# Router logits of four token tiles at once on four column tiles, turned back by a transpose; the feed-forward stage written out without a loop

## The chip, the cores and the metric

The kernel runs on one core of a Trainium2 chip. The metric is the device time in microseconds (us) of one execution, the median of three. The engines that the text speaks of are PE (TensorE, matmuls), PEld (its weight loads), DVE (VectorE), ACT (ScalarE), POOL (GpSimd) and SP (SyncE, which starts transfers). Each engine works through its own instructions strictly in the order written and waits on semaphores for the others.

## The reference

Eight sequences of 1024 tokens with 128 channels pass through a Mamba2 mixer with a small feed-forward layer, then through a top-2 mixture of eight experts. The part that the change touches is the end of the first block and the router's product:

```python
    # end of the first block, h = 128 channels a token
        out = y + residual
        h = layernorm(out, ln_w, ln_b)
        h = jax.nn.relu(h @ mlp_w1 + mlp_b1) @ mlp_w2 + mlp_b2   # 128 -> 512 -> 128
        return h + out
    ...
    x = x + _layernorm(_L0_attn_ref(...))
    # second block: the router sees the normalised x
        x = x_btd.reshape(N, Dm)                                  # _layernorm(x), 8192 tokens
        probs = jax.nn.softmax(x @ Wr + br, axis=-1)              # Wr is 128 x 8
        gates, ids = jax.lax.top_k(probs, K)
```

## The kernel before

The program is a row of stages; at the end of each all engines meet. The first builds the normalised and transposed x, the second is the scan of the mixer, and the third, whose tiles are named `m_...`, is the feed-forward stage that the change rewrites. After it come routing (`r_...`) and the experts (`e_...`).

The feed-forward stage handles 8192 tokens as 64 tiles of 128, two tiles (a group, g = 0 to 31) at a time. A group goes through a chain of steps on four engines. The order of work on each engine is a software pipeline: every engine has a list of pairs (lag, step), and in iteration i it runs, in the order of its list, each step for group i - lag. The 32 groups with a largest lag of 13 make 45 iterations. `skewed` writes iterations 0 to 15 out with constant waits and addresses, then runs iterations 16 to 31 as a hardware loop over a body of eight iterations (so the loop turns back once, after iteration 23), and writes the last 13 out again. In the loop the values of waits and some addresses come from registers.

The lists, in the order of each engine, with the lines of the program before:

- ACT: `centre_x` (lag 0, L1159, writes `m_res`), three square roots `root` (lags 1, 7, 10, L1150, `m_sd`), `turned` (3, L1165, `m_hT` from PSUM `m_pT`), `turned_xl` (12, L1179, `m_xlT` from `m_pX`), `relus` (4, L1172, four of them, `m_h` from `m_pH`).
- DVE: `mlp_out` (6, L1242, `m_at` from `m_pM`), `residual` (0, L1229, two instructions, `m_h` from `arena` and `m_res`), three sets of `bn_stats` and `bn_aggr` (L1195, L1203), three reciprocals (L1263), `apply0`, `apply1`, `apply2` (lags 2, 8, 11, all at L1209, writing `m_hn`, `m_un`, `m_xl`), `logit` (13, L1257, `logits` from `m_pL`).
- PE: `down` (5, L1296, 16 passes into `m_pM`), `up` (3, L1287, 8 passes into `m_pH`), `route` (12, L1311, 4 passes into `m_pL`), `turn` (2, L1278, `m_pT`), `turn_xl` (11, L1304, `m_pX`).
- POOL: `residual_bias` (0, L1128), `add_x` (8, L1132, `arena` from `m_un`), `keep` (11, L1136).

A float32 matmul shows in the trace as two MATMUL records (two passes), a transpose as one. Numbers are dropped from the names of tiles: `m_h<-arena` is the residual `h0`, `m_h<-m_pH` the hidden layer `h1`. Each of PSUM `m_pT`, `m_pX`, `m_pL`, `m_pH` has one copy, most tiles in SBUF four.

The waits between the engines that the prediction uses: `residual(g)` waits for `centre_x(g)`; `turn(g)` for `apply0(g)`; `turn_xl(g)` for `apply2(g)`; `up(g)` for `turned(g)`; `route(g)` for `turned_xl(g)` and for `logit(g-1)`, which empties `m_pL`.

Of the kernel before, what the change touches and what calls it, by code (L numbers as in the profile page):

```python
# [27 lines left out]
ALU = mybir.AluOpType  # L28
ACT = mybir.ActivationFunctionType
AX = mybir.AxisListType  # L30

P = 128
# [64 lines left out]
def build(nc, x, ln_w, ln_b, in_proj_w, conv_w, conv_b, dt_bias, A_log, D_skip, rms_w, out_proj_w,  # L97
# [4 lines left out]
    with ExitStack() as ctx:  # L102
        ctx.enter_context(nc.allow_non_contiguous_dma(reason="columns of a few hundred biases, one element a partition"))

        def sb(name, shape, dt=F32):
            return ctx.enter_context(nc.sbuf_tensor(name, shape, dt))
# [38 lines left out]
        w_m2 = sb("w_m2", [P, NF, D])  # L145
        w_r = sb("w_r", [P, EXPERTS])
        mean = sb("mean", [P, TILES])
# [21 lines left out]
        with ExitStack() as st:  # L169
# [51 lines left out]
            def _(sp):  # L221
                for g in range(STEPS):
# [12 lines left out]
                         (w_m2[:, :, :], mlp_w2.rearrange("(c p) d -> p c d", p=P)),  # L235
                         (w_r[:, :], Wr)]
                assert len(loads) == LOADS
# [13 lines left out]
            def _(g_):  # L251
# [12 lines left out]
                def keep(ap, base, step, chan, cmp=ALU.is_ge, fill=0.0):  # L264
                    nonlocal n
                    g_.affine_select(out=ap, in_=ap, compare_op=cmp, fill=fill, base=base,
                                     pattern=[[step, ap.shape[-1]]], channel_multiplier=chan).then_inc(s_mask, 1)
                    n += 1
                    g_.wait_ge(s_mask, n)
# [31 lines left out]
                for c in range(P // CHUNK):  # L301
                    part = causal[:, CHUNK * c:CHUNK * (c + 1)]
                    keep(part, CHUNK * c, 1, -1)
                    keep(part, -CHUNK * c, 0, 1)
                halo(STEPS - 3)
                halo(STEPS - 2)
# [755 lines left out]
        with ExitStack() as st:  # L1062
# [7 lines left out]
            def pst(name, shape=[P, 512]):  # L1070
# [15 lines left out]
            xlT = sbt("m_xlT", [P, NB, N])  # L1086
            pT, pX, pM0, pM1, pL = (pst("m_" + n) for n in ("pT", "pX", "pM0", "pM1", "pL"))
            pM = [pM0, pM1]
# [5 lines left out]
                 "xlT", "pl", "lg", "hn", "extra"))  # L1094
            s_ph2 = sem("m_ph2")
            s_extra2 = sem("m_extra2")
            s_st = [sem(f"m_st{i}") for i in range(3)]
# [6 lines left out]
            def skewed8(eng, stages):  # L1104

                skewed(eng, GROUPS, 8, 16, stages)

# [35 lines left out]
            def _(a):  # L1143
# [32 lines left out]
                def turned_xl(g, m):  # L1176
                    need(a, s_px, g)
                    need(a, s_pl, g, NB)
                    a.activation(xlT[:, m % NB, :], pX[:, 0:N], ACT.Copy).then_inc(s_xlT, 1)  # L1179

                a.activation(sd_y[:, :], ssq[:, :], ACT.Sqrt, bias=eps[:, 0:1], scale=1.0 / INNER).then_inc(s_extra2, 1)
                a.wait_ge(s_r, 2)
                skewed8(a, [(0, centre_x), (1, root(0)), (7, root(1)), (10, root(2)), (3, turned), (12, turned_xl), (4, relus)])

            @block.vector
            def _(v):
# [68 lines left out]
                def logit(g, m):  # L1255
                    need(v, s_pl, g)
                    v.tensor_tensor(tiles(logits, g), pL[:, 0:G * EXPERTS].rearrange("p (a e) -> p a e", e=EXPERTS),  # L1257
                                    brow[:, :].unsqueeze(1).broadcast_to([P, G, EXPERTS]), ALU.add).then_inc(s_lg, 1)
                def invert(n):
# [13 lines left out]
            def _(pe):  # L1273
# [32 lines left out]

                def route(g, m):
                    need(pe, s_xlT, g)
                    need(pe, s_lg, g, 1)
                    for i in range(G):  # L1310
                        ins = pe.matmul(pL[:, EXPERTS * i:EXPERTS * (i + 1)], xlT[:, m % NB, P * i:P * (i + 1)], w_r[:, :], start=True, stop=True)  # L1311
                    ins.then_inc(s_pl, 1)
                skewed8(pe, [(5, down), (3, up), (12, route), (2, turn), (11, turn_xl)])

# [552 lines left out]
```

## Time and profile before

| | us |
|---|---|
| median of three runs | 945.03 (944.18 to 947.79) |
| the profiled execution's own time | 947.09 |
| its span, first to last instruction | 945.4 |
| the feed-forward stage in it, first `m_res` to last `logits` | 365.4 to 536.4 |
| mean granted TensorE clock | 0.835 |

Over the whole span PE is busy for 71%, DVE for 70%, POOL for 49% and ACT for 48%. These shares mix stages with different limits, so the stage itself has to be read: its order by time on each engine, and what ended each wait. Times in rows of a timeline are us from the start of the span.

### The profile page before, as it was taken

How to read it: one execution, taken by the hardware profiler on the slowest of the kernel's cores; microseconds unless marked ns; L12 is line 12 of the kernel's file. 1: busy time of each engine (PE TensorE's matmuls, PEld its weight loads, DVE VectorE, ACT ScalarE, POOL GpSimd, SP SyncE). 2: the span in 40 equal slices, each digit the busy share in tenths (PEclk: the TensorE clock that was granted, in tenths of full speed). 3: DMA queues.
4: the chain of work that ended last, by engine and by line, in shares of the span. 5: the costliest groups of instructions: out<-in, count | busy, mean ns of one | idle time of the engine just before them, and what ended most of it. 6: DMA issues, size and time to landing. Idle time of an engine off the chain costs nothing. (4 is left out here: it accounts for less than half of the span.)

```text
span 945.4 us, 15492 instructions
## 1 busy us (share of the span) xinstructions
PE 670.3 (71%) x4133; PEld 532.5 (56%) x4133; DVE 663.1 (70%) x2367; ACT 455.4 (48%) x1170; POOL 461.1 (49%) x550
## 2 busy tenths in 40 slices
PE   7456999999999993999899411128498777786000
PEld 3225677777777762989899301114397666675000
DVE  7656999999999963699898586789243233332595
ACT  4764566766667654788775200016243323232143
POOL 7502666766667662234333410000577777777233
PEclk8876999999999996999999555555699999989555
DMA  9920000000000005000000057000323222211882
GB/s 218 367 89 1 1 1 1 1 2 1 1 2 1 1 1 154 26 2 2 2 0 1 1 84 98 0 0 0 91 74 76 75 73 75 75 51 50 228 245 71
DMA packets 73232, 52.95 MB, mean 56 GB/s; under 512 B 11744, under 2 KB 67048, under 8 KB 72896
## 3 DMA queue, kind: packets, MB, share of 16 engines
q1 hardware_dynamic: 67312, 41.61, 16.6%
q0 software_dynamic: 5120, 10.37, 4.1%
q8 instruction: 32, 0.52, 0.2%
q14 instruction: 48, 0.39, 0.1%
q10 hardware_dynamic: 720, 0.05, 0.1%
HBM read 28.04 MB, written 24.18 MB: 55 GB/s over the span
## 5 line engine op out<-in xcount | busy, mean ns | idle before, releaser
L817 DVE SCALAR_TENSOR_TENSOR s_cv<-s_pU,tap_w,s_cv 128x256 f32<-128x256 f32 x384 | 159.6, 477 | 20.0 <-ACT s_cv L761 19.6
L1709 POOL DMA_INDIRECT e_xg<-token_rows,token_of x80 | 82.0, 1025 | 143.3 <-issue 137.5
L1768 ACT ACTIVATE e_h<-e_pH,e_b 128x256 f32<-128x256 f32 x160 | 64.8, 470 | 123.5 <-PE e_pH L1744 123.5
L1716 POOL DMA_INDIRECT choice_rows<-e_yo,choice_of x80 | 80.6, 1007 | 25.6 <-issue 19.9
L637 POOL TENSOR_TENSOR s_xa<-s_xt,arena 128x512 f32<-128x512 f32 x32 | 34.4, 1076 | 103.1 <-ACT s_xt L779 103.1
L1754 PE MATMUL e_pO<-e_w,e_h 128*128 128x128 f32 x640 | 82.4, 285 | 0.0
L666 PE MATMUL s_pU<-arena,w_in 128*128 128x262 f32 x256 | 72.3, 407 | 11.8 <-DVE s_cv L817 8.4
L1744 PE MATMUL e_pH<-e_xgT,e_w 128*128 128x256 f32 x320 | 79.4, 393 | 1.2 <-DVE e_xgT L1800 1.2
L761 ACT ACTIVATE s_cv<-s_pU,tap_b,tap_w 128x256 f32<-128x256 f32 x128 | 65.6, 560 | 28.2 <-PE s_pU L666 27.6
L1754 PEld LDWEIGHTS e_pO<-e_w,e_h 128*128 128x128 f32 x640 | 78.9, 201 | 0.1
L1800 DVE COPY e_xgT<-e_pT 128x256 f32<-128x256 f32 x40 | 17.0, 425 | 86.7 <-PE e_pT L1734 86.7
L1287 PE MATMUL m_pH<-m_hT,w_m 128*128 128x256 f32 x256 | 64.9, 399 | 2.1 <-ACT m_h L1172 1.5
L1440 ACT ACTIVATE r_digits<-r_here,r_own 128x320 bf16<-128x320 bf16 x32 | 18.0, 562 | 99.4 <-DVE r_here L1581 99.4
L1744 PEld LDWEIGHTS e_pH<-e_xgT,e_w 128*128 128x128 f32 x320 | 60.5, 200 | 8.8 <-issue 1.8
L1296 PE MATMUL m_pM<-w_m,m_h 128*128 128x128 f32 x512 | 63.5, 278 | 0.0
L1296 PEld LDWEIGHTS m_pM<-w_m,m_h 128*128 128x128 f32 x512 | 60.6, 194 | 0.3 <-issue 0.3
L666 PEld LDWEIGHTS s_pU<-arena,w_in 128*128 128x128 f32 x256 | 45.4, 199 | 20.7 <-DVE s_cv L817 11.0
L1132 POOL TENSOR_TENSOR arena<-arena,m_un 128x256 f32<-128x256 f32 (+1 forms) x32 | 22.5, 702 | 64.8 <-DVE m_un L1209 64.8
L1287 PEld LDWEIGHTS m_pH<-m_hT,w_m 128*128 128x128 f32 x256 | 48.9, 202 | 8.8 <-ACT m_hT L1165 2.9
L1172 ACT ACTIVATE m_h<-m_pH,b_col 128x256 f32<-128x256 f32 x128 | 50.1, 484 | 0.0
L1806 DVE TENSOR_TENSOR e_ysum<-e_pO,e_b 128x256 f32<-128x256 f32 x40 | 17.0, 425 | 45.8 <-PE e_pO L1754 42.5
L1734 PE MATMUL e_pT<-ident,e_xg 128*128 128x128 f32 x80 | 17.1, 297 | 43.7 <-DMA e_xg<-token_rows,token_of 42.7
(265 smaller groups left out, 1833.2 us busy)
## 6 DMA issues: line engine op xcount, KB each, us to landing
choice_rows<-zrow SPq DMA_DIRECT2D x16, 512.0 KB, 6.6
arena<-choice_rows SPq DMA_DIRECT2D x32, 256.0 KB, 4.9
token_rows<-arena SPq DMA_DIRECT2D x8, 520.0 KB, 13.3
n_x<-in_L_attn_x_dram SPq DMA_DIRECT2D x8, 512.0 KB, 7.6
arena<-in_L_attn_x_dram SPq DMA_DIRECT2D x8, 512.0 KB, 4.6
e_w<-in_L_ffn_W_dram SPq DMA_DIRECT2D x16, 256.0 KB, 3.5
out_dram<-arena SPq DMA_DIRECT2D x16, 256.0 KB, 2.3
decay_rows<-arena SPq DMA_DIRECT2D x2, 1024.0 KB, 4.8
```

Source lines behind the costliest of these rows:

```text
L637: g.tensor_tensor(heads(xa[:, p % 3, :]), heads(xt[:, p % 2, :]), spread(pre, p), ALU.mult).then_inc(s_xa, 1)
L666: pe.matmul(pU[m % 2][:, 0:G2 * XBLK], w_in[:, P * m:P * (m + 1)], xT[:, G2 * p:G2 * (p + 1), :].rearrange("p t c -> p (t c)"), start=True ...
L761: a.activation(by_tile(cv[:, p % 2, m, :]), columns(m)[:, :, 0:P], ACT.Identity, bias=tap_b[:, m:m + 1], scale=tap_w[:, m, 0:1]).then_inc( ...
L817: v.scalar_tensor_tensor(out=by_tile(cv[:, p % 2, m, :]), in0=columns(m)[:, :, tap:tap + P], scalar=tap_w[:, m, tap:tap + 1], in1=by_tile( ...
L1172: ins = a.activation(h1[:, m % NB, c, :], pH[half_][:, N * (c % 2):N * (c % 2 + 1)], ACT.Relu, bias=b1_col[:, c:c + 1])
L1287: ins = pe.matmul(pH[half_][:, N * c:N * (c + 1)], w_m1[:, P * f:P * (f + 1)], hT[:, m % NB, :], start=True, stop=True)
L1296: ins = pe.matmul(pM[m % 2][:, P * i:P * (i + 1)], h1[:, m % NB, c, P * i:P * (i + 1)], w_m2[:, c, :], start=(c == 0), stop=(c == NF - 1))
L1709: g.indirect_dma_start(xg[:, n % RING, i, :], None, table, bass.IndirectOffsetOnAxis(ap=token_of[:, G * n + i:G * n + i + 1], axis=0), bou ...
L1716: g.indirect_dma_start(choice, bass.IndirectOffsetOnAxis(ap=choice_of[:, G * n + i:G * n + i + 1], axis=0), yo[:, n % RING, i, :], None, b ...
L1744: ins = pe.matmul(pH[n % 2][half_][:, ROWS * c:ROWS * (c + 1)], we1[:, expert(n), P * f:P * (f + 1)], xgT[:, n % 2, :], start=True, stop=True)
L1754: ins = pe.matmul(pO[n % 2][:, P * i:P * (i + 1)], hb[:, n % 2, c, P * i:P * (i + 1)], we2[:, expert(n), c, :], start=(c == 0), stop=(c == ...
L1768: ins = a.activation(hb[:, n % 2, f, :], pH[n % 2][half_][:, ROWS * c:ROWS * (c + 1)], ACT.Silu, bias=be1[:, expert(n), f:f + 1])
```

## The change

Three things change, all in the feed-forward stage apart from one fill.

The loop goes: `skewed8` now writes all 45 iterations out, so that all waits and addresses are constants.

The router's product is turned round. Before, `route` ran for each group and took each transposed tile as the stationary operand and the 8 columns of `w_r` as the moving one, which gave logits with tokens on partitions. Now `w_r` is padded with zeros to 32 columns (one more `memset` on POOL in the first stage) and is stationary, and the four transposed tiles of two groups move, each against its own 32 columns of the array, into its own 32 partitions of `m_pL`. This runs in every second iteration, for odd g. The logits then have experts on partitions, so ACT copies the 128 x 128 block to `m_lgT` (`routed`, lag 12, at the end of ACT's list), PE transposes it into the new PSUM tile `m_pK` (`route_back`, lag 13, between `turn` and `turn_xl`), and DVE adds the bias for four tiles in one instruction (`logit`, lag 13, odd g only).

The waits follow: `route` waits for the previous `routed` and no longer for `logit`; `routed` waits for `route` of the same g, in the same iteration; `route_back` for `routed`; `logit` for `route_back` of the same g, in the same iteration.

```diff
-        w_r = sb("w_r", [P, EXPERTS])
+        w_r = sb("w_r", [P, HEADS])
...
+                g_.memset(w_r[:, EXPERTS:HEADS], 0.0)
...
             def skewed8(eng, stages):
-                skewed(eng, GROUPS, 8, 16, stages)
+                for i in range(GROUPS + max(lag for lag, _ in stages)):
+                    for lag, stage in stages:
+                        if 0 <= i - lag < GROUPS:
+                            stage(i - lag, (i - lag) % 8)
...
                 def turned_xl(g, m):
                     need(a, s_px, g)
-                    need(a, s_pl, g, NB)
+                    if g // 2 >= NB // 2:
+                        need(a, s_pl, g // 2 - NB // 2)
                     a.activation(xlT[:, m % NB, :], pX[:, 0:N], ACT.Copy).then_inc(s_xlT, 1)
+                def routed(g, m):
+                    if g % 2 == 0:
+                        return
+                    q = g // 2
+                    need(a, s_pl, q)
+                    need(a, s_plT, q, 2)
+                    a.activation(lgT[:, q % 2, :], pL[:, 0:P], ACT.Copy).then_inc(s_lgT, 1)
...
-                skewed8(a, [(0, centre_x), (1, root(0)), (7, root(1)), (10, root(2)), (3, turned), (12, turned_xl), (4, relus)])
+                skewed8(a, [(0, centre_x), (1, root(0)), (7, root(1)), (10, root(2)), (3, turned), (12, turned_xl), (4, relus), (12, routed)])
...
                 def logit(g, m):
-                    need(v, s_pl, g)
-                    v.tensor_tensor(tiles(logits, g), pL[:, 0:G * EXPERTS].rearrange("p (a e) -> p a e", e=EXPERTS),
-                                    brow[:, :].unsqueeze(1).broadcast_to([P, G, EXPERTS]), ALU.add).then_inc(s_lg, 1)
+                    if g % 2 == 0:
+                        return
+                    q = g // 2
+                    need(v, s_plT, q)
+                    v.tensor_tensor(logits[:, 4 * q:4 * q + 4, :], pK[:, 0:P].rearrange("p (a e) -> p a e", e=HEADS)[:, :, 0:EXPERTS],
+                                    brow[:, :].unsqueeze(1).broadcast_to([P, 4, EXPERTS]), ALU.add).then_inc(s_lg, 1)
...
                 def route(g, m):
+                    if g % 2 == 0:
+                        return
+                    q = g // 2
                     need(pe, s_xlT, g)
-                    need(pe, s_lg, g, 1)
-                    for i in range(G):
-                        ins = pe.matmul(pL[:, EXPERTS * i:EXPERTS * (i + 1)], xlT[:, m % NB, P * i:P * (i + 1)], w_r[:, :], start=True, stop=True)
+                    need(pe, s_lgT, q, 1)
+                    for k in range(4):
+                        h, i = g - 1 + k // 2, k % 2
+                        ins = pe.matmul(pL[32 * k:32 * k + 32, 0:P], w_r[:, :], xlT[:, h % NB, P * i:P * (i + 1)], start=True, stop=True)
                     ins.then_inc(s_pl, 1)
-                skewed8(pe, [(5, down), (3, up), (12, route), (2, turn), (11, turn_xl)])
+                def route_back(g, m):
+                    if g % 2 == 0:
+                        return
+                    q = g // 2
+                    need(pe, s_lgT, q)
+                    need(pe, s_lg, q, 1)
+                    pe.transpose(pK[:, 0:P], lgT[:, q % 2, :], ident[:, :]).then_inc(s_plT, 1)
+                skewed8(pe, [(5, down), (3, up), (12, route), (2, turn), (13, route_back), (11, turn_xl)])
```

On PE, one full iteration of the middle of the stage stands like this in the program before; every iteration is the same:

```order
L1296 MATMUL m_pM<-w_m,m_h 128x128 x8
L1287 MATMUL m_pH<-m_hT,w_m 128x256 x4
L1311 MATMUL m_pL<-w_r,m_xlT 128x8 x2
L1278 MATMUL m_pT<-ident,m_hn 128x128 x2
L1304 MATMUL m_pX<-ident,m_xl 128x128 x2
```

After the change two iterations, an odd one and the even one behind it, make the pattern:

```order
L1314 MATMUL m_pM<-w_m,m_h 128x128 x8
L1305 MATMUL m_pH<-m_hT,w_m 128x256 x4
L1334 MATMUL m_pL<-m_xlT,w_r 32x128 x4
L1296 MATMUL m_pT<-ident,m_hn 128x128 x2
L1322 MATMUL m_pX<-ident,m_xl 128x128 x2
L1314 MATMUL m_pM<-w_m,m_h 128x128 x8
L1305 MATMUL m_pH<-m_hT,w_m 128x256 x4
L1296 MATMUL m_pT<-ident,m_hn 128x128 x2
L1343 MATMUL m_pK<-ident,m_lgT 128x128
L1322 MATMUL m_pX<-ident,m_xl 128x128 x2
```

Four matmuls per two groups have become four others and a transpose: the product stands behind `up` of odd iterations, the transpose back behind `turn` of even ones.

On ACT, in the same place, the iteration ends with the four `relus` and the next begins with `centre_x`:

```order
L1165 ACTIVATE m_hT<-m_pT,lnb,lnw 128x256
L1179 ACTIVATE m_xlT<-m_pX 128x256
L1172 ACTIVATE m_h<-m_pH,b_col 128x256 x4
L1159 ACTIVATE m_res<-arena,m_mm,rstd 128x128 x2
L1150 ACTIVATE m_sd<-m_mv,eps 128x2 x3
```

After the change the copy of the turned logits stands between them in odd iterations:

```order
L1171 ACTIVATE m_hT<-m_pT,lnb,lnw 128x256
L1186 ACTIVATE m_xlT<-m_pX 128x256
L1178 ACTIVATE m_h<-m_pH,b_col 128x256 x4
L1194 ACTIVATE m_lgT<-m_pL 128x128
L1165 ACTIVATE m_res<-arena,m_mm,rstd 128x128 x2
L1156 ACTIVATE m_sd<-m_mv,eps 128x2 x3
```

`m_lgT` waits for PE's product of the same iteration, and `m_res`, `m_sd` and `m_hT` of the next iteration are queued behind it.

## Rows read from the trace of the kernel before

**Rows 1.** The page: the span and each engine's busy time.
```profile
span 945.4 us, 15492 instructions
PE 670.3 (71%) x4133; PEld 532.5 (56%) x4133; DVE 663.1 (70%) x2367; ACT 455.4 (48%) x1170; POOL 461.1 (49%) x550
```

**Rows 2.** Timeline, iterations 12 to 14, written out: start, length, engine, line, [idle <-releaser].
```profile
408.37 0.61 DVE L1229 SCALAR_TENSOR_TENSOR m_h<-arena,m_rooty,m_res 128x128 f32<-128x128 f32 x2
...
411.67 0.96 DVE L1209 TENSOR_SCALAR m_xl<-arena,m_mv,m_rs 128x128 f32<-128x128 f32 x2
...
411.82 0.73 POOL L1132 TENSOR_TENSOR arena<-arena,m_un 128x256 f32<-128x256 f32 x1 [2.03 <-DVE m_un L1209]
...
412.32 0.41 PE L1278 MATMUL m_pT<-ident,m_hn 128*128 128x128 f32 x2
...
412.69 0.44 PE L1304 MATMUL m_pX<-ident,m_xl 128*128 128x128 f32 x2
...
412.77 0.56 ACT L1165 ACTIVATE m_hT<-m_pT,lnb,lnw 128x256 f32<-128x256 f32 x1 [0.98 <-PE m_pT L1278]
...
412.89 0.61 DVE L1229 SCALAR_TENSOR_TENSOR m_h<-arena,m_rooty,m_res 128x128 f32<-128x128 f32 x2
...
412.97 1.95 PE L1296 MATMUL m_pM<-w_m,m_h 128*128 128x128 f32 x16
...
414.75 1.89 PE L1287 MATMUL m_pH<-m_hT,w_m 128*128 128x256 f32 x8
...
414.92 0.90 ACT L1159 ACTIVATE m_res<-arena,m_mm,rstd 128x128 f32<-128x128 f32 x2
...
417.49 0.60 DVE L1229 SCALAR_TENSOR_TENSOR m_h<-arena,m_rooty,m_res 128x128 f32<-128x128 f32 x2
```

**Rows 3.** Timeline, the same steps inside the loop.
```profile
433.59 1.89 PE L1287 MATMUL m_pH<-m_hT,w_m 128*128 128x256 f32 x8
...
434.36 0.59 DVE L1209 TENSOR_SCALAR m_xl<-arena,m_mv,m_rs 128x128 f32 x2
...
434.81 0.69 POOL L1132 TENSOR_TENSOR arena<-arena,m_un 128x256 f32 x1 [2.04 <-DVE m_un L1209]
...
435.32 0.51 PE L1311 MATMUL m_pL<-w_r,m_xlT 128*128 128x8 f32 x4
...
435.68 0.41 PE L1278 MATMUL m_pT<-ident,m_hn 128*128 128x128 f32 x2
...
436.15 1.95 PE L1296 MATMUL m_pM<-w_m,m_h 128*128 128x128 f32 x16
```

**Rows 4.** Timeline around iteration 24, where the loop turns back.
```profile
464.17 0.42 DVE L1242 TENSOR_TENSOR m_at<-m_pM,m_h0b 128x256 f32<-128x256 f32 x1 [2.88 <-issue]
...
469.60 2.98 PE L1296 MATMUL m_pM<-w_m,m_h 128*128 128x128 f32 x16
...
472.37 2.56 PE L1287 MATMUL m_pH<-m_hT,w_m 128*128 128x256 f32 x8
```

**Rows 5.** Busy time by stretch: PE, PEld, DVE, ACT, POOL, granted clock, DMA.
```profile
470.00:480.00 10.00, 10.00 (x63) 9.39 (x63) 8.94 (x53) 6.85 (x23) 3.77 (x7) 0.83 0.00 1
...
700.00:800.00 100.00, 81.48 (x527) 72.11 (x526) 33.51 (x141) 33.48 (x83) 77.11 (x76) 0.97 0.32 80
```

**Rows 6.** Timeline of the first stage: its product on four column tiles.
```profile
26.52 1.07 PE L327 MATMUL n_pR<-arena,w_dt 128*32 128x512 f32 x8 [0.24 <-ACT arena L417]
```

**Rows 7.** Groups of instructions, 390 to 545 us: count, busy us, mean ns, idle before.
```profile
L1179 ACT ACTIVATE m_xlT<-m_pX 128x256 f32<-128x256 f32 x32 | 12.0, 376 | 14.8 <-PE m_pX L1304 14.8
```

**Rows 8.** Timeline, the end of the stage: iteration 31, and the last groups.
```profile
501.49 0.38 PE L1304 MATMUL m_pX<-ident,m_xl 128*128 128x128 f32 x2
...
530.34 0.60 DVE L1209 TENSOR_SCALAR m_xl<-arena,m_mv,m_rs 128x128 f32<-128x128 f32 x2
...
534.07 0.67 PE L1304 MATMUL m_pX<-ident,m_xl 128*128 128x128 f32 x2
...
536.27 0.17 DVE L1257 TENSOR_TENSOR logits<-m_pL,brow 128x16 f32<-128x16 f32 x1 [1.84 <-PE m_pL L1311]
```

More of the change, by code:

```diff
@@ L235, in _ @@
                          (w_m2[:, :, :], mlp_w2.rearrange("(c p) d -> p c d", p=P)),
-                         (w_r[:, :], Wr)]
+                         (w_r[:, 0:EXPERTS], Wr)]
                 assert len(loads) == LOADS
@@ L1086, in build @@
             xlT = sbt("m_xlT", [P, NB, N])
-            pT, pX, pM0, pM1, pL = (pst("m_" + n) for n in ("pT", "pX", "pM0", "pM1", "pL"))
+            lgT = sbt("m_lgT", [P, 2, P])
+            pT, pX, pM0, pM1, pL, pK = (pst("m_" + n) for n in ("pT", "pX", "pM0", "pM1", "pL", "pK"))
             pM = [pM0, pM1]
@@ L1095, in build @@
             s_ph2 = sem("m_ph2")
+            s_lgT, s_plT = sem("m_lgT"), sem("m_plT")
             s_extra2 = sem("m_extra2")
```

## The prediction, made before the changed kernel ran

> **What bounds the kernel now.** I read the page first [rows 1]: PE and DVE are both busy for about 70% of the span, so the span alone names no bound, and only the feed-forward stage is touched. Then I read that stage's timeline. In its middle PE and DVE both work almost without a break, and the skewed lists leave either little room. In the written-out part DVE is the slower: its first `m_h` of iterations 12, 13 and 14 starts at 408.37, 412.89 and 417.49 [rows 2], so an iteration costs it 4.52 us without `logit` and 4.60 with it. PE needs less. From [rows 2] `down` takes 1.78 (412.97 to 414.75); from [rows 3] `up` takes 1.73 (433.59 to 435.32), `route` 0.36 (435.32 to 435.68), and the transposes 0.47 (435.68 to 436.15): 4.34 together.
>
> Why DVE is slow there: its two `m_xl` instructions take 0.96 us while POOL's add, started at 411.82, runs beside them [rows 2]; in the loop they take 0.59, because that add starts 0.45 us after the first `m_xl` there, and no longer 0.15 [rows 3]. So the loop, whose waits go through registers, lets POOL start late, and DVE gains 0.37 us an iteration by it. Written-out code starts POOL early again.
>
> The loop has a price too. In iteration 24, where it turns back, DVE stands for 2.88 us for nothing that the profile shows, and after it PE's `m_pM` takes 2.98 instead of 1.95 and its `m_pH` 2.56 instead of 1.89 [rows 2, 4], at a granted clock of 0.83 over those ten microseconds [rows 5], a mean of its two levels. That is 2.88 + 1.03 + 0.67 = 4.58 us.
>
> I measure the middle from PE's `m_pX` of iteration 12 (412.69 [rows 2]) to that of iteration 31 (501.49 [rows 8]): 88.80 us for 19 iterations, or 84.22 without the turn, 4.43 each. From there to the end of the last `logits` (536.27 + 0.17 [rows 8]) it is 34.95 us.
>
> **The change part by part.** *The loop goes:* 4.58 us are gained. The wait disappears and not only moves, if straight code is fetched in time, for which the first 16 iterations of the same stage speak. On the other side DVE pays the 0.37 us in iterations 16 to 31 as well.
>
> *PE's work:* per pair of groups 2 x 0.36 us of `route` leave. What comes is one product on four column tiles and one transpose. The nearest row for the product is the first stage's: eight records of 512 columns in 1.07 us [rows 6], so the four tiles run beside each other; mine have a quarter of the columns and I take 0.24 us of PE's time, between 0.11 (one pass of 128 columns: 1.78 / 16 [rows 2]) and 0.9 (eight such passes in turn). The transpose is half of the 0.25 that two take (0.47 less the 0.22 to 0.28 between `m_pX` and `m_pM` [rows 2, 3]): 0.12. PE saves 0.36 us a pair. PE isn't what limits the written-out part, so in the middle this brings nothing by itself.
>
> *DVE's work:* one `logit` less in two iterations. It costs 4.60 - 4.52 = 0.08; DVE would need 9.12 a pair.
>
> *The new wait on ACT:* this is the expensive part. `m_lgT` of an odd iteration waits for the product of the same iteration, which stands behind PE's `down` and `up`. Queued behind it on ACT is `m_res` of the next iteration, and for that DVE's `m_h` waits. Before, `m_res` was done early. With DVE's first `m_h` of an even iteration as zero:
> - `m_h` to the end of `m_xl`: 411.67 + 0.96 - 408.37 = 4.26 [rows 2];
> - `turn_xl` starts 0.06 later (412.69), and `down` of the odd iteration 0.28 after that: 4.60;
> - `down` 1.78, `up` 1.73: 8.11;
> - the product until ACT can start: I take the 0.45 from the start of two transposes to `m_hT` (412.32 to 412.77 [rows 2]), as it too is two passes of 128 columns: 8.56;
> - `m_lgT` before the next ACT instruction: between 0 (hidden in the pipeline) and the 0.38 of a copy twice as wide [rows 7]; I take half, 0.20: 8.76;
> - `m_res` 0.90 [rows 2] and 0.06 to DVE: 9.72.
>
> There the next even `m_h` starts. The circle closes in 9.72 us for two iterations, more than the 9.12 of DVE and the 8.3 of PE (2 x 4.34 - 0.36). The other new waits have room. In the even iteration PE starts `down` at 4.60 + 4.32 + 0.28 - 9.72 = -0.52, so `up` at 1.26, `turn` at 2.99 and `route_back` at 3.24; its result is there 0.45 later, at 3.7, and DVE comes to `logit` after `m_xl`, at 4.26. `m_hT` stands on ACT behind `m_res` and three square roots and may be late for `up`; PE's pause before `m_pX`, from 3.36 to 4.32, takes that up.
>
> *Sum of the middle:* the first such pause is in iteration 14. `down` of iteration 13 starts at 412.97; plus 1.78, 1.73, 0.45, 0.20 and 0.96 is 418.09, where 417.49 was. Eight pairs to iteration 30: 495.85. Iteration 31 follows after 4.60, its `m_xl` ends and `turn_xl` starts 4.32 later: 504.77, against 501.49. The middle loses 3.3 us: 4.58 gained, 7.9 lost (19 iterations of 4.85 and not 4.43).
>
> *The end:* in iterations 32 to 35 there is no `m_res`, and PE is the limit; it saves 0.18 an iteration, 0.7. Then groups go through single file: the last `m_xl` is done at 530.94, but PE turns it only at 534.07, 3.1 us late [rows 8]. The product falls away for every second group, and I take half of this lag back, 1.6. Five `logit` fewer on DVE are 0.4. The last group gets a copy and a transpose more before its logits: 0.4 lost. Together 2.3 gained; bounds are 0 and 4.
>
> *The fill on POOL* lies in the first stage, where POOL ends early; nothing. Sum: +3.3 - 2.3 = **+1.0 us**. The profiled execution took 947.09, 2.06 above the median of 945.03; against it I forecast 948.1, against the median **946.0**.
>
> A rule that speaks against the change: a product on column tiles between full-array matmuls. The 1.07 us of [rows 6] don't show what the switch costs, as waits stand at both sides. By the Trainium skill (TensorEngine Tiling (Array Packing), Tiling Modes, Key Properties) a change of the tiling mode drains the engine; the next bound from rows for that is in the rivals.
>
> **The rivals.**
> - *The new circle doesn't bind* (ACT gets the product earlier, or hand-overs overlap), and DVE's 9.12 rules. Iteration 14 at 417.43, then 8 x 9.12 + 4.60 + 4.32: 499.31, 2.2 gained in the middle, and 2.3 at the end: 945.03 - 4.5 = 940.5. For it: each hand-over is a difference of single rows. Against it: it needs 0.6 us a pair, more than any one term that I chose. 0.17.
> - *The switch to column tiles drains PE.* The product then can't start before the last `up` has ended, 1.89 after its start [rows 3] and not 1.73, and its weights load only then (0.11, as one pass): 0.27 into the circle, in 9 pairs 2.4: 948.4. For it: no row shows a product that follows full-array work without a wait. Against: only that this is small. The rule of the skill named above would do just this. 0.15.
> - *The column tiles run in turn*, 0.9 us: 0.66 more in each circle, 9 x 0.66 = 5.9: 951.9. Against it [rows 6]. 0.04.
> - *Slower: PE's clock falls.* In each even iteration PE would wait nearly 1 us for `m_xl`, after `route_back`. When the clock fell once in the old loop, it cost 1.70 [rows 4]. From three falls it decides (+1.0 + 5.1: 951), with one in each pair it is 946 + 9 x 1.7 = 961. For it: PE would be busy for only 86% of the circle. Against it: from 700 to 800 us it is busy for 81% and is granted 0.97 [rows 5]. 0.07.
> - *Slower: the code isn't fetched in time.* One stop of DVE as at the loop's turn, now in straight code, gives back the 4.58: 950.6. For it: nine more iterations of code on each engine. Against it: none in the first 16. 0.09.
>
> My forecast has the remaining 0.48.
>
> **How the numbers follow.** A measurement of this kernel tells about 0.5% from no change, 4.7 us: faster is below 940.3, slower above 949.8. The forecast (with its bounds of the copy, -0.20 and +0.18 in 9 pairs, and 2 us at the end: 943 to 949.5) and the drain lie within 0.5%. Of the circle that doesn't bind I count 0.10 of 0.17 as faster, and 0.04 of the forecast's for an end that gains all 4. Slower are the tiles in turn, the clock, the late code, less a little each: 0.17. That leaves 0.69. The range takes in the circle that doesn't bind and one stop: 940 to 950.6.
>
> **What the profile would show.** Right: no [<-issue] of near 3 us on DVE; `m_xl` at 0.96 in all middle iterations; DVE idle before `m_h` of every even iteration from 14 to 30, ended by ACT `m_res`, by about 0.6 us; ACT idle before `m_lgT`, ended by PE `m_pL`; PE idle before `m_pX` in even iterations by about 0.9 us; `m_pX` of iteration 31 some 3 us later than before, counted from that of iteration 12, and the end 2.3 us shorter. Wrong: the start to start of even `m_h` at 9.1 (no circle) or above 10 (tiles in turn, or a lower clock, to be told by the lengths of `m_pL` and `m_pM`). A DVE that waits for `m_pK` would mean that I set the second new wait too early.

## The result and the profile after

| | before | after |
|---|---|---|
| median, in the same session | 945.62 us (944.18 to 947.79, 6 runs) | 950.12 us (947.73 to 951.87, 6 runs) |
| ratio, 95% interval | | 1.0045 (1.0026 to 1.0064) |
| own time of the profiled execution | 947.09 | 948.95 |
| first `m_res` to last `logits` in it | 171.06 | 173.39 |

The change costs 4.5 us. The interval leaves out 1, so the changed kernel is slower; the size is a little less than the 0.5% (4.7 us) within which the forecast called a kernel unchanged. 946.0 was forecast, with 950.6 as the upper end.

The page of the changed kernel; the rows before are [rows 1]:

```profile
span 947.2 us, 15109 instructions
PE 666.5 (70%) x4149; PEld 518.0 (55%) x4149; DVE 667.1 (70%) x2351; ACT 459.3 (48%) x1186; POOL 462.3 (49%) x551
```

PE is busy for 3.8 us less and DVE for 4.0 more. Only the second repeats: in the repeated executions of both kernels (10 and 11 below) it is 0.8 less and 4.1 more. Neither says why the stage got longer. Its timeline does, for one pair of iterations in the middle (start, length, engine, line, [idle <-releaser]):

```profile
434.43 0.42 PE L1334 MATMUL m_pL<-m_xlT,w_r 128*32 128x128 f32 x8
434.57 0.72 POOL L1138 TENSOR_TENSOR arena<-arena,m_un 128x256 f32<-128x256 f32 x1 [2.03 <-DVE m_un L1224]
...
434.79 0.44 PE L1296 MATMUL m_pT<-ident,m_hn 128*128 128x128 f32 x2
434.92 0.28 ACT L1194 ACTIVATE m_lgT<-m_pL 128x128 f32<-128x128 f32 x1 [2.05 <-PE m_pL L1334]
435.10 0.86 ACT L1165 ACTIVATE m_res<-arena,m_mm,rstd 128x128 f32<-128x128 f32 x2
...
435.99 0.61 DVE L1244 SCALAR_TENSOR_TENSOR m_h<-arena,m_rooty,m_res 128x128 f32<-128x128 f32 x2 [0.28 <-ACT m_res L1165]
...
437.14 1.56 ACT L1178 ACTIVATE m_h<-m_pH,b_col 128x256 f32<-128x256 f32 x4
...
438.11 1.97 PE L1305 MATMUL m_pH<-m_hT,w_m 128*128 128x256 f32 x8 [0.45 <-ACT m_h L1178]
...
439.29 0.97 DVE L1224 TENSOR_SCALAR m_xl<-arena,m_mv,m_rs 128x128 f32<-128x128 f32 x2
...
440.13 0.27 PE L1343 MATMUL m_pK<-ident,m_lgT 128*128 128x128 f32 x1
...
440.31 0.44 PE L1322 MATMUL m_pX<-ident,m_xl 128*128 128x128 f32 x2
...
440.44 0.19 DVE L1275 TENSOR_TENSOR logits<-m_pK,brow 128x32 f32<-128x32 f32 x1 [0.19 <-PE m_pK L1343]
...
440.58 1.95 PE L1314 MATMUL m_pM<-w_m,m_h 128*128 128x128 f32 x16
...
442.37 1.89 PE L1305 MATMUL m_pH<-m_hT,w_m 128*128 128x256 f32 x8
...
444.19 0.43 PE L1334 MATMUL m_pL<-m_xlT,w_r 128*32 128x128 f32 x8
...
444.68 0.28 ACT L1194 ACTIVATE m_lgT<-m_pL 128x128 f32<-128x128 f32 x1 [2.05 <-PE m_pL L1334]
444.86 0.87 ACT L1165 ACTIVATE m_res<-arena,m_mm,rstd 128x128 f32<-128x128 f32 x2
...
445.76 0.35 DVE L1244 SCALAR_TENSOR_TENSOR m_h<-arena,m_rooty,m_res 128x128 f32<-128x128 f32 x1 [0.28 <-ACT m_res L1165]
```

Follow the starts from 435.99 to 445.76, the two even `m_h`. DVE's `m_h` leads to its `m_xl`, which ends just before `m_pX` starts (4.32 us after the start of `m_h`). From `m_pX` it goes on to `down` (0.27), `up` (1.79), the product `m_pL` (1.82), ACT's `m_lgT` (0.49), `m_res` (0.18) and the next `m_h` (0.90): 9.77 us a pair. The circle is there, and it closes where the prediction had it.

Its sign is the [0.28 <-ACT m_res], which looks harmless. The same dependence stands in the waits as ACT's (us in total, times, longest):

```profile
ACT m_lgT L1194 <- PE m_pL L1334: 18.5, 9, 2.1
...
PE m_pH L1305 <- ACT m_h L1178: 4.3, 9, 0.8
```

These are waits from 410 to 500 us. The first row alone would not mean a loss, as ACT is busy for only 48%. It matters because `m_res` is queued behind it. The second row is a wait that the prediction did not name (below).

The bounds of the middle and the last groups, as for before in [rows 2, 8]:

```profile
411.02 0.44 PE L1322 MATMUL m_pX<-ident,m_xl 128*128 128x128 f32 x2 [0.34 <-DVE m_xl L1224]
...
503.80 0.44 PE L1322 MATMUL m_pX<-ident,m_xl 128*128 128x128 f32 x2 [0.22 <-DVE m_xl L1224]
...
531.53 1.24 DVE L1224 TENSOR_SCALAR m_xl<-arena,m_mv,m_rs 128x128 f32<-128x128 f32 x4
...
534.44 0.66 PE L1322 MATMUL m_pX<-ident,m_xl 128*128 128x128 f32 x2 [0.31 <-ACT m_xlT L1186]
...
537.14 0.19 DVE L1275 TENSOR_TENSOR logits<-m_pK,brow 128x32 f32<-128x32 f32 x1 [2.78 <-PE m_pK L1343]
```

From the first to the second the middle takes 92.78 us (88.80 before), and from there to the end of the last `logits` the end takes 33.53 (34.95 before).

### The profile page after: what moved, and what is told of

Same layout as the page of the kernel before. It is cut to its first block and busy times, and to the rows that moved or that the text cites. A ratio compares the mean times of both kernels' runs of the same rounds, so it can differ in the third digit from the quotient of the medians.

```text
span 947.2 us, 15109 instructions
## 1 busy us (share of the span) xinstructions
PE 666.5 (70%) x4149; PEld 518.0 (55%) x4149; DVE 667.1 (70%) x2351; ACT 459.3 (48%) x1186; POOL 462.3 (49%) x551
## 5 line engine op out<-in xcount | busy, mean ns | idle before, releaser
L1138 POOL TENSOR_TENSOR arena<-arena,m_un 128x256 f32<-128x256 f32 x32 | 22.9, 716 | 64.4 <-DVE m_un L1224 64.4
```

## The experiments

All kernels are read by the same two stretches: the middle, from the first `m_pX` of iteration 12 to that of iteration 31, and the end, from there to the end of the last `logits`. "Outside" is the span less the stage from first `m_res` to last `logits`. A ratio is against the kernel before on the same chip. The kernels are called by their numbers in this table.

| kernel | median us | ratio (95%) | middle | end | outside |
|---|---|---|---|---|---|
| before, profiled execution | | | 88.80 | 34.95 | 774.3 |
| 10: the same again | 945.37 | 0.9998 (0.9986 to 1.0010) | 88.79 | 34.95 | 772.7 |
| after, profiled execution | | | 92.78 | 33.53 | 773.8 |
| 11: the same again | 950.45 | 1.0043 (1.0026 to 1.0059) | 92.78 | 33.52 | 775.1 |
| 1: written out, old product | 946.13 | 1.0005 (0.9993 to 1.0017) | 87.89 | 34.95 | 774.7 |
| 2: loop, new product | 948.52 | 1.0029 (1.0020 to 1.0039) | 94.37 | 34.13 | 772.1 |
| 3: copy an iteration later | 941.46 | 0.9953 (0.9939 to 0.9967) | 86.71 | 33.34 | 772.4 |
| 4: 3 and `apply2` before `apply1` | 944.15 | 0.9982 (0.9968 to 0.9995) | 87.18 | 35.21 | 774.1 |
| 5: 3 and two fills on POOL | 943.57 | 0.9977 (0.9961 to 0.9993) | 88.07 | 33.46 | 772.0 |
| 6: 5 and `logit` later | 945.14 | 0.9991 (0.9977 to 1.0005) | 88.08 | 33.12 | 773.3 |
| 7: 3 and POOL's add waits | 940.80 | 0.9947 (0.9934 to 0.9959) | 84.27 | 34.22 | 773.7 |
| 8: 7 and `logit` later | 940.40 | 0.9941 (0.9927 to 0.9954) | 84.50 | 33.91 | 773.9 |
| 9: 1 and POOL's add waits | 942.89 | 0.9963 (0.9950 to 0.9975) | 84.32 | 35.15 | 776.9 |

**1. Only the loop goes.** The kernel before, with the new `skewed8`:

```diff
             def skewed8(eng, stages):
-                skewed(eng, GROUPS, 8, 16, stages)
+                for i in range(GROUPS + max(lag for lag, _ in stages)):
+                    for lag, stage in stages:
+                        if 0 <= i - lag < GROUPS:
+                            stage(i - lag, (i - lag) % 8)
```

> The kernel before with one part of the change alone: the feed-forward stage is written out, the router's product stays as it was. Theory (the writing out gains the loop's turn and loses the late start of POOL's add; the new wait on ACT is what costs): no 2.9 us stop of DVE, every m_xl pair at 0.96 us, DVE at 4.58 us an iteration, so m_pX of iteration 12 to m_pX of iteration 31 in 19 x 4.58 = 87.0 us against 88.8 before and 92.8 after the whole change; the end as before, 35.0; total 1.8 us below the kernel before, some 6 below the changed one. Rival (written-out code is what costs, by fetching or by the port that DVE and POOL share): 4 us above the kernel before, as the whole change.

DVE's `m_h` of two iterations, in its timeline:

```profile
457.59 0.60 DVE L1232 SCALAR_TENSOR_TENSOR m_h<-arena,m_rooty,m_res 128x128 f32<-128x128 f32 x2
462.17 0.60 DVE L1232 SCALAR_TENSOR_TENSOR m_h<-arena,m_rooty,m_res 128x128 f32<-128x128 f32 x2
```

Each iteration takes 4.58 us with no stop of DVE, in place of 4.43 and one stop. The middle is 0.9 shorter than before, and not 1.8 as expected: 18 of its 19 steps take near 4.58, but from iteration 12 to 13 `m_pX` takes 5.37 (411.53 to 416.90), as it took 5.38 in the kernel before, where PE's `route` waits once for `logit`. The saved turn of the loop and the slower `m_xl` nearly cancel, and the median can't be told from before; the 1.8 us less that were expected of it are not seen.

**2. Only the new product.** The loop is kept, with the new product, copy and transpose in its body; the semaphores of the product's steps count by 2. Against the changed kernel (the lines for the counting by 2 are left out here):

```diff
-                for i in range(GROUPS + max(lag for lag, _ in stages)):
-                    for lag, stage in stages:
-                        if 0 <= i - lag < GROUPS:
-                            stage(i - lag, (i - lag) % 8)
+                skewed(eng, GROUPS, 8, 16, stages)
```

> The changed kernel with the loop kept for iterations 16 to 31; its semaphores of the router's steps count by two, so that waits in the loop follow from the group number. Theory (the circle over ACT's copy costs): inside the loop the circle is 9.76 - 0.37 = 9.4 us a pair, as m_xl isn't held by POOL there, and the loop's turn costs its 4.6 again: m_pX of iteration 12 to 31 in 19.5 + 15 x 4.7 + 4.6 = 94.6 us; the end 33.5; total 4.3 above the kernel before and 1.8 above the changed one. Rival (the writing out is what costs): equal to the kernel before within 1 us.

DVE's `m_h` in its loop, for one pair and the next even iteration:

```profile
478.49 0.61 DVE L1239 SCALAR_TENSOR_TENSOR m_h<-arena,m_rooty,m_res 128x128 f32<-128x128 f32 x2 [0.83 <-ACT m_res L1162]
483.39 0.61 DVE L1239 SCALAR_TENSOR_TENSOR m_h<-arena,m_rooty,m_res 128x128 f32<-128x128 f32 x2
488.30 0.61 DVE L1239 SCALAR_TENSOR_TENSOR m_h<-arena,m_rooty,m_res 128x128 f32<-128x128 f32 x2 [0.69 <-ACT m_res L1162]
```

A pair takes 9.81 us here with `m_xl` at 0.60. The circle of the prediction should have become 0.37 shorter, 9.4, and it did not; DVE only waits the longer for `m_res` (0.7 to 0.8 in place of 0.28). PE's and DVE's rows of the same pair say what holds it:

```profile
480.44 1.97 PE L1299 MATMUL m_pH<-m_hT,w_m 128*128 128x256 f32 x8 [0.83 <-ACT m_h L1175]
...
481.78 0.60 DVE L1219 TENSOR_SCALAR m_xl<-arena,m_mv,m_rs 128x128 f32 x2
...
482.46 0.27 PE L1335 MATMUL m_pK<-ident,m_lgT 128*128 128x128 f32 x1
482.57 0.38 PE L1316 MATMUL m_pX<-ident,m_xl 128*128 128x128 f32 x2
```

`m_xl` has ended at 482.38, 0.19 before `m_pX` starts, so `m_pX` no longer waits for DVE. It stands behind PE's own list: `up` (`m_pH`), `turn` and `route_back`, and `up` waits for ACT's `relus` (`m_h`), which are queued behind the same copy. This is a second circle: copy, `relus`, `up`, `turn`, `route_back`, `turn_xl`, `down`, `up`, product, copy. It doesn't pass through DVE, and here it is the longer one.

The sum of the middle came out near the expected 94.6 by luck. A pair takes 0.4 us more than expected, and the turn of the loop 0.6 (the pair with it takes 10.43, from `m_h` at 458.17 to `m_h` at 468.60) and not 4.6. The middle is 5.6 us longer than before. So the new product with its copy slows the stage without the writing out, and the missing loop gives part of it back.

**3. The copy an iteration later.** One entry of ACT's list of the changed kernel moves, so that nothing on ACT waits behind a product of the same iteration:

```diff
-                skewed8(a, [(0, centre_x), (1, root(0)), (7, root(1)), (10, root(2)), (3, turned), (12, turned_xl), (4, relus), (12, routed)])
+                skewed8(a, [(0, centre_x), (1, root(0)), (7, root(1)), (10, root(2)), (13, routed), (3, turned), (12, turned_xl), (4, relus)])
```

> The changed kernel with ACT's copy of the turned logits one iteration later in ACT's list, behind the three square roots and ahead of m_hT (lag 13 and not 12), where the product has long been there. Nothing else is changed. Theory (the circle product, copy, m_res, m_h, m_xl, m_pX, down, up sets 9.76 us a pair): the circle is cut, DVE's 9.12 us a pair is the bound; m_pX of iteration 12 to 31 in 19 x 4.56 = 86.6 us against 92.8; total 6 us below the changed kernel and 1.5 to 3.5 below the kernel before. Rival (the extra time comes from the column tiles, the transpose back or the instruction fetch): equal to the changed kernel within 1 us. Second rival (DVE's wait for m_pK takes over at once): 2 to 3 us below the changed kernel, with DVE idle before logits.

ACT, and then DVE, in its timeline:

```profile
449.42 0.90 ACT L1165 ACTIVATE m_res<-arena,m_mm,rstd 128x128 f32<-128x128 f32 x2
...
451.61 0.28 ACT L1194 ACTIVATE m_lgT<-m_pL 128x128 f32<-128x128 f32 x1 [0.75 <-PE m_pL L1334]
```
```profile
450.82 0.96 DVE L1224 TENSOR_SCALAR m_xl<-arena,m_mv,m_rs 128x128 f32<-128x128 f32 x2
...
456.66 0.60 DVE L1244 SCALAR_TENSOR_TENSOR m_h<-arena,m_rooty,m_res 128x128 f32<-128x128 f32 x2
461.16 0.61 DVE L1244 SCALAR_TENSOR_TENSOR m_h<-arena,m_rooty,m_res 128x128 f32<-128x128 f32 x2
465.77 0.60 DVE L1244 SCALAR_TENSOR_TENSOR m_h<-arena,m_rooty,m_res 128x128 f32<-128x128 f32 x2
```

`m_res` now runs 2.2 us ahead of the copy. Both waits are gone, DVE's for `m_res` and for `m_pK`, and a pair takes 9.11 us (456.66 to 465.77): what DVE needs. The middle falls by 6.1 us against the changed kernel and the median by about 9. So the copy's place in ACT's list was the loss. The edit takes `m_res` and the `relus` out from behind the copy at once, and with them both circles; no run takes away one alone. DVE is now the bound, with `m_xl` at 0.96. The median is 4.1 us below the kernel before, more than the 1.5 to 3.5 expected; the stage itself is 4.0 shorter (171.06 to 167.05).

**4. `m_xl` away from POOL's add by the order of DVE.** To kernel 3:

```diff
-                            (7, invert(1)), (1, invert(0)), (2, apply0), (8, apply1), (11, apply2), (13, logit)])
+                            (7, invert(1)), (1, invert(0)), (2, apply0), (11, apply2), (8, apply1), (13, logit)])
```

> The kernel with the later copy, and on DVE m_xl ahead of m_un in each iteration, so that POOL's add (which m_un releases) no longer starts in the middle of m_xl. Theory (POOL's add holds the second m_xl for 0.37 us in each iteration): m_xl pairs at 0.59 us; if nothing else is held in its place DVE needs 4.2 us an iteration, m_pX of iteration 12 to 31 in about 80 us, 12 below the changed kernel. If the add then holds m_h, which also reads two tiles from SBUF, the 0.37 us come back there: m_h pairs near 0.9 to 1.0 us, and the total is that of the kernel with the later copy alone. Rival (m_xl is slow for another reason): m_xl pairs stay at 0.96 us.

DVE, then POOL, in its timeline:

```profile
437.33 0.59 DVE L1224 TENSOR_SCALAR m_xl<-arena,m_mv,m_rs 128x128 f32<-128x128 f32 x2
...
438.79 0.96 DVE L1244 SCALAR_TENSOR_TENSOR m_h<-arena,m_rooty,m_res 128x128 f32<-128x128 f32 x2
```
```profile
438.51 0.69 POOL L1138 TENSOR_TENSOR arena<-arena,m_un 128x256 f32<-128x256 f32 x1 [2.55 <-DVE m_un L1224]
439.14 0.46 POOL L1142 COPY arena<-m_xl 128x256 f32<-128x256 f32 x1
```

`m_xl` is at 0.59, but the add now falls onto `m_h`, which takes 0.96 in place of 0.60. The contention moved and didn't go. The middle is 0.5 longer than kernel 3's and the end 1.9. The second branch of the expectation had the contention right, but not its total: the median is 2.7 above kernel 3's, and what lengthens the end was not looked for.

**5 and 6. The add later by two small fills; and `logit` behind `residual`.** The first edit is made to kernel 3 and gives kernel 5, the second is made to kernel 5 and gives kernel 6:

```diff
                     need_apart(g_, s_un, g)
+                    g_.memset(pause[:, 0:1], 0.0)
+                    g_.memset(pause[:, 1:2], 0.0)
                     g_.tensor_tensor(tiles(x1, g), rows[:, bass.ds(G * g, G), 0:D], un[:, m % NB], ALU.add).then_inc(s_x1, 1)
```
```diff
-                skewed8(v, [(6, mlp_out), (0, residual), (9, statistics(2, of_x1)), (6, statistics(1, of_at)),
+                skewed8(v, [(6, mlp_out), (0, residual), (14, logit), (9, statistics(2, of_x1)), (6, statistics(1, of_at)),
...
-                            (7, invert(1)), (1, invert(0)), (2, apply0), (8, apply1), (11, apply2), (13, logit)])
+                            (7, invert(1)), (1, invert(0)), (2, apply0), (8, apply1), (11, apply2)])
```

> The kernel with the later copy, and between POOL's wait for m_un and its add two fills of one column each, so that the add starts about 0.2 us later, as it did in the loop, when the second m_xl is already under way. Theory (the add holds whichever VectorE instruction starts after it on the port that both use, and only its moment counts): m_xl pairs at 0.59 us, the second m_h of a pair at 0.48 instead of 0.34 as in the loop, DVE at 4.3 us an iteration; then DVE's wait for m_pK (behind turn on PE) is close to binding at 8.7 us a pair: m_pX of iteration 12 to 31 in 83 us against 86.7; total 3 to 4 below the kernel with the later copy. Rival (the 0.37 us come back elsewhere, as when m_xl was moved ahead of m_un): 86 to 87 us, the same total.

> The same, and DVE's logit one iteration later (lag 14, behind the two m_h), so that it never waits for m_pK. Theory (in the kernel with the later add the wait for m_pK binds): 19 x 4.3 = 82 us or less in the middle, down to the 80 of PE; total 1 to 3 below that kernel. Rival (DVE's own work binds there already): equal within 0.5 us.

POOL, then DVE, in the timeline of kernel 5:

```profile
443.41 0.10 POOL L1139 MEMSET m_pause<- 128x1 f32 x1 [2.02 <-DVE m_un L1227]
443.44 0.10 POOL L1140 MEMSET m_pause<- 128x1 f32 x1
443.49 0.76 POOL L1141 TENSOR_TENSOR arena<-arena,m_un 128x256 f32<-128x256 f32 x1
```
```profile
443.27 1.06 DVE L1227 TENSOR_SCALAR m_xl<-arena,m_mv,m_rs 128x128 f32<-128x128 f32 x2
```

Two fills delay the add by only 0.08 us. It starts 0.22 after the first `m_xl`, still ahead of the second, which is held until the add has ended at 444.25 and ends itself at 444.33: longer, not shorter. This delay is too small and makes it worse: the middle is 1.4 longer than kernel 3's. Both the expectation and its rival are missed. With `logit` moved (6) the middle is the same, so nothing there hung on `m_pK`.

**7 to 9. The add waits for the first `m_xl`.** The edit is made to kernel 3 and gives kernel 7; with `logit` moved as in 6 it gives kernel 8; made to kernel 1, which has the old product, it gives kernel 9:

```diff
+                        if n == 2 and i == 0:
+                            ins.then_inc(s_xlh, 1)
...
                     need_apart(g_, s_un, g)
+                    need(g_, s_xlh, g - 3)
```

> The kernel with the later copy; the first m_xl instruction of each pair signals a new semaphore when it ends, and POOL's add waits for that too. So the add starts about 0.4 us after the first m_xl has started, as in the loop of the kernel before, while the second m_xl is under way. The two fills of the kernel with the later add put it off by 0.08 us only. Theory (the add holds the VectorE instruction that starts after it until it ends): m_xl pairs at 0.59 us, m_h pairs at 0.75 as in the old loop, DVE at 4.3 to 4.4 us an iteration, m_pX of iteration 12 to 31 in 82 to 84 us against 86.7; total 3 to 4 below the kernel with the later copy. Rival (the 0.37 us come back whatever the moment): 86 to 88 us.

> The same, and DVE's logit one iteration later (lag 14, behind the two m_h). Theory (with a faster DVE its wait for m_pK, behind turn on PE, binds at about 8.7 us a pair): 1 us or more below the kernel with the add after the first m_xl. Rival: DVE's own work still binds, equal within 0.5 us in the middle.

> The kernel before, written out, with the same wait of POOL's add for the first m_xl, and the router's product as it was. It tells what the new product is worth where DVE no longer leaves PE room. PE needs 4.34 us an iteration here and 4.16 with the new product. Theory: DVE at 4.4 (with a logit in every iteration), PE waits little; m_pX of iteration 12 to 31 in 83 to 84 us against 87.9 without the wait, 4 us below the kernel before in the middle, within 1 us of the kernel with the new product; the end 35.0 us against its 33.3. Rival (the contention goes elsewhere): 87 to 88 us.

DVE, then POOL, in the timeline of kernel 7:

```profile
443.47 0.59 DVE L1226 TENSOR_SCALAR m_xl<-arena,m_mv,m_rs 128x128 f32<-128x128 f32 x2
...
444.32 0.86 DVE L1248 SCALAR_TENSOR_TENSOR m_h<-arena,m_rooty,m_res 128x128 f32<-128x128 f32 x2
```
```profile
443.95 0.68 POOL L1140 TENSOR_TENSOR arena<-arena,m_un 128x256 f32<-128x256 f32 x1 [2.35 <-DVE m_xl L1226]
```

DVE's `m_h` over a pair of kernel 7, then over an iteration of kernel 9:

```profile
466.61 0.74 DVE L1248 SCALAR_TENSOR_TENSOR m_h<-arena,m_rooty,m_res 128x128 f32<-128x128 f32 x2
470.88 0.86 DVE L1248 SCALAR_TENSOR_TENSOR m_h<-arena,m_rooty,m_res 128x128 f32<-128x128 f32 x2
475.45 0.74 DVE L1248 SCALAR_TENSOR_TENSOR m_h<-arena,m_rooty,m_res 128x128 f32<-128x128 f32 x2
```
```profile
466.32 0.78 DVE L1236 SCALAR_TENSOR_TENSOR m_h<-arena,m_rooty,m_res 128x128 f32<-128x128 f32 x2
470.72 0.78 DVE L1236 SCALAR_TENSOR_TENSOR m_h<-arena,m_rooty,m_res 128x128 f32<-128x128 f32 x2
```

The add now starts 0.48 after the first `m_xl`, as it did in the loop (0.45 [rows 3]), and `m_xl` takes 0.59. A part comes back at `m_h` (0.74 and 0.86). A pair takes 8.84 us, and the middle 84.27, 8.5 less than with the change as made and 2.4 less than kernel 3's. The expected 3 to 4 us do not show in the time of the whole: the stage is 1.8 shorter than kernel 3's (165.27 to 167.05), and the ratios 0.9947 and 0.9953 can't be told apart. With the old product the gain is clear of the noise: 0.9963 for kernel 9 against 1.0005 for kernel 1. An iteration takes 4.40 there and the middle 84.32, the same as with the new product. So in the middle the new product earns nothing even when its copy is well placed; it shows at the end, by 0.9 us (34.22 against 35.15), and the intervals of the two ratios (7 and 9) still overlap. Moving `logit` (8) changes nothing that can be told.

**10 and 11. Both kernels again, unchanged.**

> The kernel before once more, unchanged, for a second trace: how far its parts move from one execution to the next. Expected: the feed-forward stage within 0.5 us of the first trace, the stage of the experts within 3 us.

> The changed kernel once more, unchanged. Its medians are 4 us above the kernel before, its feed-forward stage in the first trace only 2.3 us longer. If the other 2 us come with the code (its place, its fetching), the part behind the stage is again near 410 us against 409 before; if they are chance of the executions, it moves by as much either way. The stage itself again 173 us.

Middle and end repeat within 0.01 us, "outside" does not: 1.6 us between two executions of the kernel before, 1.3 between two after. The part behind the stage is 409.9 in both executions of the changed kernel, as expected if its cost came with the code, and 409.0 and 407.7 in those of the kernel before; in kernels 1 to 9 it lies anywhere from 406.8 to 410.4. That decides nothing.

## Why the prediction was right, and where it was off

*The forecast and its range.* The mechanism was right: the new wait on ACT closes a circle, and the stage gets longer by it. The size was not: +1.0 us was forecast and +4.5 measured. The range holds the measured 950.12 only because its upper end, 950.6, was set for a rival, one stop of DVE in straight code, and no such stop is in the trace. That the measured time lies in the range is, in this part, luck. What is missing from the +1.0 is taken apart below: 0.7 in the middle, 0.9 at the end, and the rest outside the stage.

*The loop's turn.* Right: DVE has no stop in straight code, `m_xl` stands at 0.97 again, and kernel 1 takes 4.58 us an iteration where 4.60 was forecast for DVE with `logit`. (The rival of the late code spoke of nine more iterations of code; 45 against 16 + 8 + 13 are eight.)

*The circle.* Right in mechanism and size: 9.77 where 9.72 was forecast. By terms: `m_h` to `m_pX` 4.32 (4.32), to `down` 0.27 (0.28), `down` 1.79 (1.78), `up` to the product 1.82 (1.73), to the copy 0.49 (0.45), the copy 0.18 (0.20), `m_res` to `m_h` 0.90 (0.96). That the place of the copy was the loss is shown by kernel 3. What kernel 3 does not show is that this circle alone was, since it removes a second one too (under *The other waits*).

*The switch to column tiles.* The rival said 0.27 more a circle; the row says 0.09 (1.82 less 1.73). PE's time for the product is 0.36 (434.43 to 434.79), and I took 0.24, from the first stage's product. By the rule of the Trainium skill (TensorEngine Tiling (Array Packing), Tiling Modes, Key Properties) the switch drains the engine; if these two surpluses (0.09, and 0.36 less 0.24) are that drain, it costs about 0.1 us at each side. That is an estimate, and no run separates it from other causes. The eight passes take 0.42 with their ends, against 1.95 for the 16 of `m_pM`, so the tiles don't run in turn.

*The other waits.* Here a step failed. I wrote that "the other new waits have room" and looked only at `m_hT` and `route_back`. ACT's four `relus` are queued behind the same copy, and `m_pH` has one copy in PSUM. In even iterations `up` waits for them, `[0.45 <-ACT m_h]`, and `route_back` behind it is late. I had put its result at 3.7 us behind the even `m_h`, half a microsecond before DVE comes for it; DVE could start only at 440.44 - 435.99 = 4.45, after a wait. The prediction's own sign for this, "a DVE that waits for m_pK", is in the trace. Each odd `m_h` comes 4.90 after the even one (440.89 after 435.99 here) and not 4.60. This is why DVE waits for `m_res` by 0.28 us and not by the 0.6 of the prediction, and why PE's idle time is not the 0.9 before even `m_pX` that it gave as a sign: it is 0.45 before `m_pH`, and 0.21 before the odd `m_pX`.

What the step overlooked is a second circle, almost as long as the first. In the changed kernel the even `m_pX` starts 0.05 after `m_xl` has ended (440.31, 440.26) and 0.18 after `m_pK`; in kernel 2, where it doesn't wait for DVE, it starts 0.11 after `m_pK`. So the way through `relus` has some 0.07 us of room here, which makes it an estimated 9.70 a pair beside 9.77. A faster `m_xl`, which shortens the first circle alone, would gain no more than that by this estimate, and kernel 2 gained nothing by it. The cost came out right since the two happen to be so near each other.

*The middle.* It took 92.78 against the forecast 92.08: about 9 times 0.05 for the longer circle, and 0.3 for the step from iteration 30 to 31, 4.90 and not 4.60.

*The end.* 1.4 us were gained, and 2.3 forecast. The lag of the last `m_pX` behind the last `m_xl` is 534.44 - 532.77 = 1.67; before it was 3.13, so half of it came back, as taken. The last group's way from `m_pX` to the end of `logits` is 2.89, after 2.37 before the change: 0.5 lost where 0.4 was forecast. What failed is the remainder. From iteration 31 to the end of the last `m_xl` it takes 28.97 us, after 29.45 before: 0.5 gained where PE's saving and five `logit` fewer were to give 1.1.

*The clock.* It did not fall in the stage's middle, in spite of PE's waits:

```profile
410.00:500.00 90.00, 83.52 (x600) 70.02 (x599) 85.47 (x447) 67.79 (x211) 34.36 (x56) 1.00 0.01 2
```

These are the busy us of PE, PEld, DVE, ACT and POOL from 410 to 500 us, then the granted clock: 1.00, the upper level, with PE busy for 93% (the prediction's rival had 86%).

*The sum.* The stage became 2.3 us longer in the profiled executions and 2.6 in the repeated ones (170.86 to 173.46), where 1.0 was forecast. The medians differ by 4.5 and 4.3 (5.1 between kernels 11 and 10), so some 2 us more lie outside the stage, and the prediction had nothing there. Single executions say little of it (kernel 9's profiled one took 944.94, its median is 942.89), so I take each median less the time around the span (1.7, in kernels 5 and 6 2.0) and less the stage, which repeats within 0.2: 772.9 before, 775.0 after, 774.4 for kernel 1 and 771.0 for kernel 2; kernels 3 to 9 have 772.6 to 774.9 (the kernel before had medians of 945.6 to 946.3 beside these). The two with the loop are low, which would fit a cost of the longer code outside its stage; but kernels 3 and 5 are written out too and have 772.7 and 772.6. This stays open; no run separates it.

Both kernels are beaten by kernel 3, written out with the copy an iteration later (0.9953), and by kernels 7 and 8, which have POOL's add behind the first `m_xl` besides (0.9947 and 0.9941). These three can't be told apart by their times; by its own timeline the stage of kernels 7 and 8 is 1.8 and 1.9 us shorter than that of kernel 3.

## What to carry to other kernels

A wait at the end of an engine's list holds what stands at the head of the next iteration. Close the circle through every engine before calling it hidden, and do so for each step queued behind the wait, not for the first alone; list each single-copy buffer that these steps set free. When a step needs a result of the same iteration from a busy engine, give it one iteration more of lag: here one entry moved in one list was worth about 9 us, twice the whole effect of the change. When two engines hold each other up, moving the holder must be checked against what it lands on next.

## What the runs showed of the hardware

DVE held by POOL. By the Trainium skill (SBUF — State Buffer, section SBUF: two separate sides) GpSimd and a VectorE operation that works in a two-port mode or has two inputs in SBUF share a port pair as an exclusive lock: whichever starts first has it for the whole instruction, and the other is fully blocked. For a VectorE instruction that comes second the traces agree: `m_xl` ends 0.09 us after POOL's add in the changed kernel (435.38, 435.29) and 0.08 in kernel 5, where the add took 0.72 and 0.76. That POOL is held in the same way is not shown: in kernel 7 the add starts while the second `m_xl` should be under way, and takes 0.68. The start decides: an add 0.16 or 0.22 after the first of two `m_xl` costs 0.38 or 0.47 us, one 0.48 after it nothing there. What was unexpected is a reason for the old loop's speed: it delays POOL's add, and kernel 7 gets the same delay by one semaphore. What in the loop delays it is not shown. The prediction named its waits through registers, but in the loop `need_apart` also puts a semaphore instruction (`sem_inc` on `carrier`) between the wait and the add, which the written-out code doesn't have.
